# Three k columns of a graph layer's attention moved among its first batches, and three orders in the count sweeps

## Chip, cores and metric

One Trainium2 chip, one core. The metric is the device time of one launch in microseconds, the median of several executions.

## What is computed

Four graph layers over 512 nodes of 512 features and 8704 edges (src, dst, type, weight), each with a residual and a layer norm around it. Two of them are attentions. Layer 0 has a dense score bias with the edge weights; layer 1 is a graph convolution by degree; layer 2 sums messages by relation; layer 3 is attention over the edges:

```python
q = (h @ Wq).reshape(n, H, DK)
k = (h @ Wk).reshape(n, H, DK)
v = (h @ Wv).reshape(n, H, DK)
e = jnp.einsum('ehd,ehd->eh', k[src], q[dst]) / np.sqrt(DK).astype(np.float32)
...
a = jax.ops.segment_sum(attn[:, :, None] * v[src], dst, num_segments=n)
```

with 8 heads of 64. Because there are few nodes, the kernel works with dense 512 x 512 matrices: it counts the edges between each pair of nodes, and an edge that occurs c times enters layer 3's softmax as a bias log c on the dense score.

## The kernel before, in words

**Precision.** Every product of float32 matrices is three products: each operand is split into a high half (`th`, `wh`, `qh`, `kh`, rounded to the matrix format) and a low half (the rest), and low x high, high x low and high x high are added in one PSUM bank (`product`). A result that is needed as an operand is cast by ScalarE (`high`), and VectorE subtracts to get the low half (`part_low`, L1438), which frees the bank. The weights' high halves are DMA copies issued from GpSimd's queue (`cast`, L371; three slots, so a copy waits for the last product with the weight that was in its slot, `W_LAST`); their low halves are GpSimd subtractions (`low`, L379) of a copy that SyncE's queue loads in quarters.

**Count sweeps.** The edges come in 68 chunks of 128. For each chunk VectorE builds one-hot tiles (`build_chunk`: the source, and the destination with a digit for the type) in a ring of four slots, and TensorE multiplies them into eight banks, 8 products of 128 x 512 a chunk (`chunk`, `sweep`). There are two sweeps, of 8 and 9 blocks of 4 chunks. In between, ScalarE copies banks 0 to 3 out and VectorE banks 4 to 7 (L1373), and the second sweep starts each bank with one product (L596) once it is free. From the third block on VectorE also marks duplicate edges: `mark` compares the keys of one chunk with those behind it, `settle` writes the cell of two chunks (`cell_at`), and GpSimd scatters the edge weights of these cells to DRAM (L444). Before the first loop VectorE also computes `second` and splits the bias rows into `add2` (`bias_rows`), between the chunks of its third block. The one-hot tiles are compared with `iota`, a row of numbers that is loaded by ScalarE's queue (L987); the edges `ei` are the first load of SyncE's queue (L299), and VectorE's first wait.

**Attention** (`attention`, one function on each engine, called for layers 0 and 3). An item m of 32 is one head and one of four row tiles. Its steps:
- scores, in banks 0 to 3, two items at a time (TensorE, L670)
- bias added and row peak taken, which frees the score bank (VectorE `peak_of`, L1479)
- exponent with row sum (ScalarE `exponent`, L955), reciprocal of the sum (VectorE `inverse_of`)
- scaling (GpSimd `scale_rows`, L403)
- four transposes of 128 x 128, in banks 4 to 6 (TensorE `probT`, L679)
- copy of the transposed row out of its bank: even items ScalarE (`even_row`), odd items VectorE (`odd_row`)
- the product with v, when all rows of a head pair are there, in bank 7 or 3 (TensorE, L692).

Every queue is written out by hand in batches b = 0 to 8 of four items: batch b on TensorE holds the scores of items 4b to 4b+3, the transposes of items 4b-4 to 4b-1, and then value products. Scores of batch b need the banks that the peaks of batch b-1 free. Head pair p (items 8p to 8p+7) uses column p of q and k: column 1 from batch 2, column 2 from batch 4, column 3 from batch 6. `psum_plan` (L67) gives each result its bank and its turn in it.

**Layer 3 before the attention.** After v, TensorE makes q columns 0 to 3 (banks 0 to 3) and k columns 0 to 3 (banks 4 to 7), 12 products each (L871, L872); ScalarE and VectorE follow with the halves in the same order. GpSimd's queue holds here the low halves of the output weight, then `cast(19)` and `cast(20)` (L510, L511; the two weights of the last feed-forward step), then `scale_rows`, which has the low halves of weights 19 and 20 behind items 4, 7, 10, 13, 16 and 19.

Of the kernel before, what the change touches and what calls it, by code (L numbers as in the profile page):

```python
# [22 lines left out]
ALU = mybir.AluOpType  # L23
# [43 lines left out]
def psum_plan():  # L67
# [47 lines left out]
    tiles("k3", 4)  # L115
# [26 lines left out]
def build(nc, x0, x0t, row_ids_d, edges, edge_rows, edge_w, weights, rows_of, cols_of, rel_b, ident_d, iota_d, later_d, out):  # L142
# [6 lines left out]
    with ExitStack() as ctx:  # L149
# [147 lines left out]
        def _(sp_):  # L297
            eng = sp_
            eng.dma_start(ei[:], edges.rearrange("a p c -> p a c")).then_inc(s["ld_edge"], 16)  # L299
# [68 lines left out]
        def _(pool):  # L368
# [28 lines left out]
            def scale_rows(a, base, mask, work):  # L397

                for m in range(ITEMS):
# [7 lines left out]
                    if a == 0 and m == 11:  # L407
                        cast(5)
# [102 lines left out]
            cast(20)  # L511
# [9 lines left out]
        def _(pe):  # L521
# [103 lines left out]

            def rows(name, w, ready, ks=K):
# [28 lines left out]
            def attention(a, base):  # L655
                first, v_done = 4 * (a // 3), 4 * (a // 3 + 1)
                for b in range(BATCHES + 2):
# [16 lines left out]
                    for t in range(4 * b - 4, 4 * b):  # L674
                        if 0 <= t < ITEMS:
# [195 lines left out]
            columns("q3", 16, lambda i: None)  # L871
            columns("k3", 17, lambda i: None)  # L872
# [43 lines left out]
        def _(act):  # L916
# [33 lines left out]
            def attention(a, base):  # L950
# [16 lines left out]
                for b in range(BATCHES + 1):  # L967
# [8 lines left out]
                    if b:  # L976
                        even_row(4 * b - 2)
                    if b < BATCHES:
                        exponent(4 * b + 2)
                        exponent(4 * b + 3)  # L980
                for p in range(2, HEADS // 2):
                    mixed(a, p)
# [4 lines left out]
            act.dma_start(iota[:], iota_d.to_broadcast([P, 2 * N])).then_inc(s["ld_iota"], 16)  # L987
# [175 lines left out]
            for f in range(K):  # L1163
                high(("q3", f), qh[:, f, :], s["q_high"])
            for f in range(K):
                high(("k3", f), kh[:, f, :], s["k_high2"])
# [33 lines left out]
        def _(dve):  # L1200
# [144 lines left out]
            for slot in range(RING):  # L1345
                dve.wait_ge(s["hot_used1"], FIRST_PLACED * RING + slot - RING + 1)
                build_chunk(FIRST_PLACED * RING + slot, slot)
                if slot == 1:
                    dve.wait_ge(s["ld_ident"], 16)
                    link(dve.tensor_reduce(second[:], ident[:, 1::32], AX_X, ALU.add))  # L1350
                    link(dve.tensor_scalar(second[:], second[:], -1.0, None, ALU.mult))
                if slot == 2:
                    dve.wait_ge(s["ld_bias"], 64)
                    bias_rows(rows[:], slice(0, P), 0)
# [10 lines left out]
            before, behind = CBLOCKS[0] * RING, (CBLOCKS[0] - FIRST_PLACED) * RING  # L1365
            dve.wait_ge(ld_keys[2], 16)
            dve.wait_ge(ld_keys[3], 16)
            for slot in range(RING - 1):
                dve.wait_ge(s["hot_used1"], before - RING + slot + 1)
                build_chunk(before + slot, slot)  # L1370
            for i in range(T):
# [3 lines left out]
            for k in range(GROUP):  # L1375
                mark(behind, k)
                if k % 2:
                    settle(behind, behind // GROUP, k // 2)
# [91 lines left out]
            def attention(a, base):  # L1470
# [26 lines left out]
                for b in range(BATCHES + 1):  # L1497
                    if b:
                        inverse_of(4 * b - 1)
# [372 lines left out]
```

## Time and profile before

| | us |
|---|---|
| median of 3 executions | 529.7 (529.44 to 530.45) |
| profiled execution, its own time | 532.03 |
| its span, first to last instruction | 530.1 |
| TensorE busy in the span | 503.2 |
| VectorE busy | 382.8 |
| GpSimd busy | 277.7 |
| ScalarE busy | 225.7 |

The profile is that of one execution. A row gives the start, the duration, the engine and line, the operation, output and input with their shapes, and in brackets the idle time before it with what ended it. PE is TensorE, DVE VectorE, ACT ScalarE, POOL GpSimd, SP SyncE; a q behind the name is the engine's own queue, where DMAs are issued. Matrix products overlap, so one that lasts 0.39 us is followed by the next after some 0.22 us.

### The profile page before, as it was taken

Reading aid. Unit: us, or ns where it says so; the run is one execution under the profiler, and the core shown is the slowest. Engines: PE = TensorE matmul, PEld = TensorE weight load, DVE = VectorE, ACT = ScalarE, POOL = GpSimd, SP = SyncE. Lnnn points to the kernel's source line nnn. Section 1 sums busy time; section 2 is a strip of 40 time slices with the busy share of each in tenths; the row PEclk is TensorE's granted clock in tenths of the full one; section 3 lists DMA queues with packets and bytes.
Section 4 is the critical chain, followed back from the end, with each engine's and each line's share of the span. In section 5 each row is a group of like instructions: output and inputs, shape, how many; then the busy total and the mean of one; then the engine's idle time right before and its main releaser. Section 6 shows DMA issues by size and latency. Waiting matters only on the chain.

```text
span 530.1 us, 7860 instructions
## 1 busy us (share of the span) xinstructions
PE 503.2 (95%) x2483; PEld 344.5 (65%) x2498; DVE 382.8 (72%) x972; ACT 225.7 (43%) x474; POOL 277.7 (52%) x283
## 2 busy tenths in 40 slices
PE   7999999999999899999999999999999999899992
PEld 2444444444786564787788888889888786565771
DVE  5999979999986776977654863764348625776586
ACT  2102370004614776557461244435535225776365
POOL 5877777777403989402552544523532752867101
PEclk9999999999999999999999999999999998999998
DMA  6923410000293441050853564322453853100002
GB/s 192 354 74 108 113 28 1 0 0 2 85 355 100 133 122 61 4 176 19 246 155 104 183 187 137 124 80 80 131 172 97 254 163 88 52 0 1 2 0 79
DMA packets 32409, 56.48 MB, mean 107 GB/s; under 512 B 5152, under 2 KB 8686, under 8 KB 31864
## 3 DMA queue, kind: packets, MB, share of 16 engines
q1 hardware_dynamic: 19276, 31.35, 19.1%
q0 software_dynamic: 11728, 18.92, 12.0%
q10 hardware_dynamic: 1372, 5.81, 3.0%
q8 instruction: 17, 0.28, 0.2%
q14 instruction: 16, 0.13, 0.1%
HBM read 51.79 MB, written 4.26 MB: 106 GB/s over the span
## 4 chain that ended last, share of the span: by engine, by line
PE 70%; POOL 9%; DVE 7%; issue 6%; DMA 5%; ACT 4%; POOLq 0%; DVEq 0%; ACTq 0%
PE bank L563 12%; PE bank L564 12%; PE bank L565 12%; PE bank L586 11%; PE bank L692 4%; PE bank L783 3%; PE bank L782 3%; POOL wl L389 3%; PE bank L679 3%; DMA edge_bias<-nbias 3%; POOL sp L403 2%; PE bank L670 2%; PE bank L644 2%; POOL edge_bias L444 1%; DVE sp L1479 1%
## 5 line engine op out<-in xcount | busy, mean ns | idle before, releaser
L389 POOL TENSOR_TENSOR wl<-wraw,wh 128x512 fp32r<-128x512 f32 (+1 forms) x78 | 102.1, 1324 | 71.6 <-DMA wh<-w 15.5
L586 PE MATMUL bank<-hot 128*128 128x512 bf16 x514 | 114.3, 379 | 4.3 <-DVE hot L1303 3.4
L586 PEld LDWEIGHTS bank<-hot 128*128 128x128 bf16 x528 | 51.2, 98 | 67.5 <-DVE hot L1303 6.4
L444 POOL DMA_INDIRECT edge_bias<-ew,cell_at x68 | 71.1, 1046 | 30.3 <-issue 17.7
L563 PE MATMUL bank<-wh,tl 128*128 128x512 f32 x176 | 69.5, 395 | 0.1
L565 PE MATMUL bank<-wh,th 128*128 128x512 f32 x176 | 68.8, 391 | 0.0
L564 PE MATMUL bank<-wl,th 128*128 128x512 f32 x176 | 68.7, 390 | 0.0
L1303 DVE TENSOR_SCALAR hot<-iota,pair_dst,digit 128x1024 bf16<-128x1024 f16 x68 | 41.9, 616 | 0.2 <-issue 0.2
L955 ACT ACTIVATE sp<-sp,peak 128x512 f32<-128x512 f32 x44 | 31.8, 723 | 23.6 <-DVE peak L1479 23.2
L1302 DVE TENSOR_SCALAR hot<-iota,ef 128x512 bf16<-128x512 f16 x68 | 37.7, 554 | 4.9 <-PE bank L586 3.9
L1284 DVE SCALAR_TENSOR_TENSOR eq<-keyb,key,later 128x384 f16<-128x384 f16 (+1 forms) x68 | 40.1, 612 | 0.0
L563 PEld LDWEIGHTS bank<-wh,tl 128*128 128x128 f32 x176 | 33.1, 188 | 8.0 <-issue 1.3
L565 PEld LDWEIGHTS bank<-wh,th 128*128 128x128 f32 x176 | 33.0, 188 | 7.1
L564 PEld LDWEIGHTS bank<-wl,th 128*128 128x128 f32 x176 | 33.1, 188 | 6.8
L1206 DVE TENSOR_TENSOR tl<-bank,th 128x512 fp32r<-128x512 f32 x32 | 21.9, 689 | 18.1 <-ACT th L930 11.1
L940 ACT ACTIVATE gap<-h,neg 128x512 f32<-128x512 f32 x24 | 17.4, 726 | 35.9 <-DVE neg L1217 35.9
L563 PE MATMUL bank<-th,wl 128*128 128x512 f32 x80 | 31.2, 390 | 0.7 <-issue 0.7
L564 PE MATMUL bank<-tl,wh 128*128 128x512 f32 x80 | 31.2, 389 | 0.2 <-issue 0.2
L468 POOL TENSOR_SCALAR x<-h,neg,rstd 128x512 f32<-128x512 f32 x6 | 5.5, 924 | 49.2 <-DVE rstd L1266 49.1
L565 PE MATMUL bank<-th,wh 128*128 128x512 f32 x80 | 31.2, 390 | 0.0
L1479 DVE CUSTOM_DVE_ANT_0 sp<-bank,nbias 128x512 f32<-128x512 f32 x44 | 29.4, 682 | 1.3 <-PE bank L670 0.8
L692 PE MATMUL bank<-probT,v 128*64 128x512 f32 x128 | 30.1, 602 | 0.0
(239 smaller groups left out, 1062.1 us busy)
## 6 DMA issues: line engine op xcount, KB each, us to landing
wraw<-w SPq DMA_DIRECT2D x26, 256.0 KB
wh<-w POOLq DMA_DIRECT2D x6, 1024.0 KB, 6.3
keyb<-edge_keys ACTq DMA_DIRECT2D x4, 1088.0 KB, 9.7
wh<-w_rel POOLq DMA_DIRECT2D x4, 1024.0 KB, 5.9
wraw<-w_rel SPq DMA_DIRECT2D x16, 256.0 KB
wraw<-w_qkv SPq DMA_DIRECT2D x8, 256.0 KB
wh<-w_o POOLq DMA_DIRECT2D x2, 1024.0 KB, 6.8
count_rows<-counts SPq DMA_DIRECT2D x1, 2048.0 KB, 14.1
```

The source lines that it names most:

```text
L389: pool.tensor_tensor(wl[n % WSLOTS][:, k, 0:width], wraw[:, q % 3, 0:width], wh[n % WSLOTS][:, k, 0:width], ALU.subtract).then_inc(s["w_lo ...
L444: pool.indirect_dma_start(out=bias_dram, out_offset=bass.IndirectOffsetOnAxis(ap=cell_at[:, c:c + 1], axis=0), in_=ew[:, c:c + 1], in_offs ...
L563: pe.matmul(ps(name)[:], al, bh, start=start and k == 0, stop=False)
L564: pe.matmul(ps(name)[:], ah, bl, start=False, stop=False)
L565: mm = pe.matmul(ps(name)[:], ah, bh, start=False, stop=stop and k == ks - 1)
L586: mm = pe.matmul(ps(name)[:], hot[:, slot, 0, i * P:(i + 1) * P], hot[:, slot, 1 + kind, :], start=False, stop=last, skip_group_check=True)
L692: mm = pe.matmul(ps(name)[HD * e:HD * e + HD, :], v[:, j, hd * HD:(hd + 1) * HD], probT[:, hd % 4, j, :], start=j == 0, stop=j == T - 1, s ...
L955: act.activation(sp[m % SP][:], sp[m % SP][:], ACT.Exp, bias=peak[:, c:c + 1], scale=-1.0, accum_out=total[:, c:c + 1]).then_inc(s["exped" ...
L1284: return dve.scalar_tensor_tensor(out=eq[:, k, :], in0=keyb[:, bass.ds(c * P, WINDOW * P)], scalar=key[:, bass.ds(c, 1)], in1=later[:], op ...
L1302: dve.tensor_scalar(hot[:, slot, 0, :], iota[:, 0:N], ef[:, 0, bass.ds(j, 1)], None, ALU.is_equal)
L1303: dve.tensor_scalar(hot[:, slot, 1:3, :].rearrange("p a n -> p (a n)"), iota[:], pair_dst[:, bass.ds(j, 1)], digit[:, bass.ds(j, 1)], ALU. ...
L1479: frees(dve.tensor_tensor_reduce(sp[m % SP][:], ps(name)[:], nbias[:, item(m)[1], :], -HD ** -0.5, 3e38, ALU.add, ALU.min, peak[:, c:c + 1 ...
```

## The change

In layer 3, q columns 0 to 2 are followed by k column 0 and q column 3. K columns 1 to 3 are made in the attention's batches 0 to 2, on TensorE ahead of the transposes of the batch's third item (in batch 0 there is none: behind the scores), all three in bank 7. ScalarE casts column b+1 behind batch b's four exponents and moves the batch's second row copy behind that; VectorE makes the low half in the next batch, ahead of its peaks, and moves the second row copy behind the fourth peak. `cast(20)` moves from ahead of the scalings to behind the twelfth.

In the sweeps, the load of `iota` moves from ScalarE's queue to the head of SyncE's; `second` and the bias rows move from VectorE's third block to behind its first loop; and the first two marks of the next group, with their settle, move from behind the bank copies to between the second and third build of the second sweep.

```diff
@@ psum_plan
-    tiles("k3", 4)
+    for f in range(K):
+        use(("k3", f), 7 if f else 4)
@@ SyncE, head of the queue
+            eng.dma_start(iota[:], iota_d.to_broadcast([P, 2 * N])).then_inc(s["ld_iota"], 16)
@@ GpSimd, scale_rows
-                    if a == 0 and m == 11:
-                        cast(5)
+                    if m == 11:
+                        cast(5 if a == 0 else 20)
...
             cast(19)
-            cast(20)
@@ TensorE
+            def column(name, w, f):
+                begin((name, f))
+                finish(product((name, f), w_tile(w, f), t_tile()), (name, f))
@@ TensorE, attention
                     for t in range(4 * b - 4, 4 * b):
+                        if a == 3 and t == 4 * b - 2 and b < K - 1:
+                            column("k3", 17, b + 1)
@@ TensorE, layer 3
-            columns("q3", 16, lambda i: None)
-            columns("k3", 17, lambda i: None)
+            w_ready(16)
+            for f in range(K - 1):
+                column("q3", 16, f)
+            w_ready(17)
+            column("k3", 17, 0)
+            column("q3", 16, K - 1)
@@ ScalarE, attention
-                    if b:
+                    beside = a == 3 and b < K - 1
+                    if b and not beside:
                         even_row(4 * b - 2)
                     if b < BATCHES:
                         exponent(4 * b + 2)
                         exponent(4 * b + 3)
+                    if beside:
+                        high(("k3", b + 1), kh[:, b + 1, :], s["k_high2"])
+                        if b:
+                            even_row(4 * b - 2)
...
-            act.dma_start(iota[:], iota_d.to_broadcast([P, 2 * N])).then_inc(s["ld_iota"], 16)
@@ VectorE, attention
                         inverse_of(4 * b - 1)
+                    if a == 3 and 0 < b < K:
+                        part_low("k3", b, kl, kh, 0.0, s["k_high2"], s["k_ready"])
...
-                    if b:
+                    beside = a == 3 and b < K - 1
+                    if b and not beside:
                         odd_row(4 * b - 1)
                     if b < BATCHES:
                         peak_of(4 * b + 3)
                         inverse_of(4 * b + 2)
+                    if b and beside:
+                        odd_row(4 * b - 1)
@@ VectorE, sweeps
                 build_chunk(FIRST_PLACED * RING + slot, slot)
-                if slot == 1:
-                    dve.wait_ge(s["ld_ident"], 16)
-                    link(dve.tensor_reduce(second[:], ident[:, 1::32], AX_X, ALU.add))
-                    link(dve.tensor_scalar(second[:], second[:], -1.0, None, ALU.mult))
-                if slot == 2:
-                    dve.wait_ge(s["ld_bias"], 64)
-                    bias_rows(rows[:], slice(0, P), 0)
@@ VectorE, behind the first loop
+            dve.wait_ge(s["ld_ident"], 16)
+            link(dve.tensor_reduce(second[:], ident[:, 1::32], AX_X, ALU.add))
+            link(dve.tensor_scalar(second[:], second[:], -1.0, None, ALU.mult))
+            dve.wait_ge(s["ld_bias"], 64)
+            bias_rows(rows[:], slice(0, P), 0)
             dve.wait_ge(ld_keys[2], 16)
             dve.wait_ge(ld_keys[3], 16)
             for slot in range(RING - 1):
                 dve.wait_ge(s["hot_used1"], before - RING + slot + 1)
                 build_chunk(before + slot, slot)
+                if slot == 1:
+                    mark(behind, 0)
+                    mark(behind, 1)
+                    settle(behind, behind // GROUP, 0)
...
             build_chunk(before + RING - 1, RING - 1)
-            for k in range(GROUP):
-                mark(behind, k)
-                if k % 2:
-                    settle(behind, behind // GROUP, k // 2)
+            mark(behind, 2)
+            mark(behind, 3)
+            settle(behind, behind // GROUP, 1)
```

Layer 3's halves of q and k on ScalarE and VectorE outside the attention follow TensorE's new order (q 0 to 2, k 0, q 3).

## Rows read from the trace of the kernel before

**Rows 1.** The page's first part: busy time, share of the span and instructions.

```profile
PE 503.2 (95%) x2483; PEld 344.5 (65%) x2498; DVE 382.8 (72%) x972; ACT 225.7 (43%) x474; POOL 277.7 (52%) x283
```

**Rows 2.** TensorE's timeline, 0 to 84 us: start, duration, what, idle before it.

```profile
7.06 12.26 PE L586 MATMUL bank<-hot 128*128 128x512 bf16 x55 [1.37 <-DVE hot L1303]
...
29.46 34.71 PE L586 MATMUL bank<-hot 128*128 128x512 bf16 x155 [0.67 <-DVE hot L1303]
...
66.33 13.98 PE L586 MATMUL bank<-hot 128*128 128x512 bf16 x63
81.34 2.98 PE L586 MATMUL bank<-hot 128*128 128x512 bf16 x12 [1.03 <-DVE hot L1303]
```

**Rows 3.** TensorE's timeline in layer 3's attention.

```profile
441.47 0.50 PE L670 MATMUL bank<-kh,ql 64*128 64x512 f32 x2
...
447.56 3.15 PE L679 MATMUL bank<-ident,sp 128*128 128x128 f32 x16
...
455.36 0.63 PE L679 MATMUL bank<-ident,sp 128*128 128x128 f32 x4 [0.70 <-ACT probT L964]
...
462.91 0.50 PE L670 MATMUL bank<-kh,ql 64*128 64x512 f32 x2
...
464.49 2.21 PE L679 MATMUL bank<-ident,sp 128*128 128x128 f32 x16
466.64 1.94 PE L692 MATMUL bank<-probT,v 128*64 128x512 f32 x8
```

**Rows 4.** Busy time by stretch; behind it granted clock, DMA share, GB/s.

```profile
447.60:456.00 8.40, 7.28 (x47) 5.81 (x46) 6.30 (x23) 6.41 (x16) 5.71 (x8) 0.86 0.08 19
```

**Rows 5.** ScalarE's timeline, the casts of k columns 2 and 3.

```profile
438.86 0.59 ACT L925 CAST kh<-bank 128x512 fp32r<-128x512 f32 x1 [2.13 <-PE bank L565]
441.58 0.59 ACT L925 CAST kh<-bank 128x512 fp32r<-128x512 f32 x1 [2.13 <-PE bank L565]
```

**Rows 6.** VectorE's timeline, last low half of k and first peak.

```profile
442.20 0.69 DVE L1441 SCALAR_TENSOR_TENSOR kl<-bank,kh 128x512 fp32r<-128x512 f32 x1 [2.03 <-ACT kh L925]
443.15 0.69 DVE L1479 CUSTOM_DVE_ANT_0 sp<-bank,nbias 128x512 f32<-128x512 f32 x1 [0.26 <-DVE kl L1441]
```

**Rows 7.** GpSimd's timeline, weight copies and first scalings of layer 3.

```profile
436.17 0.76 POOL L377 DMA_DIRECT2D wh<-w  x1
...
445.01 1.53 POOL L403 TENSOR_SCALAR sp<-sp,scale,deg 128x512 f32<-128x512 f32 x2 [2.47 <-DVE scale L1486]
```

**Rows 8.** The page's sixth part: weight copies, KB each, us to landing.

```profile
wh<-w POOLq DMA_DIRECT2D x6, 1024.0 KB, 6.3
```

**Rows 9.** Timelines of SyncE's queue and VectorE, the first load.

```profile
0.80 0.43 SPq L299 DMA_DIRECT2D ei<-edges_in  x1
...
4.91 0.27 DVE L1275 CAST ef<-ei 128x204 f32<-128x204 int32 x1 [4.91 <-DMA ei<-edges_in]
```

**Rows 10.** VectorE's timeline, operations of the bias rows.

```profile
22.38 0.15 DVE L1350 TENSOR_REDUCE second<-ident 128x1 f32<-128x4 f32 x1
...
23.49 0.51 DVE L1338 CAST add<-rows 128x512 fp32r<-128x512 f32 x1
24.04 0.75 DVE L1340 SCALAR_TENSOR_TENSOR add<-add,second,rows 128x512 fp32r<-128x512 f32 x1
```

**Rows 11.** Timelines of VectorE and GpSimd between the count sweeps.

```profile
58.08 1.84 DVE L1302 TENSOR_SCALAR hot<-iota,ef 128x512 bf16<-128x512 f16 x1
...
60.38 0.34 DVE L1302 TENSOR_SCALAR hot<-iota,ef 128x512 bf16<-128x512 f16 x1
...
63.56 2.48 DVE L1373 COPY packed<-bank 128x512 f32<-128x512 f32 x4 [0.27 <-PE bank L586]
...
67.84 0.61 DVE L1284 SCALAR_TENSOR_TENSOR eq<-keyb,key,later 128x384 f16<-128x384 f32 x1
...
58.48 1.29 POOL L389 TENSOR_TENSOR wl<-wraw,wh 128x512 fp32r<-128x512 f32 x1
```

**Rows 12.** VectorE's timeline in the second sweep's first rounds.

```profile
79.95 0.86 DVE L1302 TENSOR_SCALAR hot<-iota,ef 128x512 bf16<-128x512 f16 x1 [3.31 <-PE bank L586]
```

More of the change, by code:

```diff
@@ L1162, in _ @@
             turned(3, 3)
-            for f in range(K):
+            for f in range(K - 1):
                 high(("q3", f), qh[:, f, :], s["q_high"])
-            for f in range(K):
-                high(("k3", f), kh[:, f, :], s["k_high2"])
+            high(("k3", 0), kh[:, 0, :], s["k_high2"])
+            high(("q3", K - 1), qh[:, K - 1, :], s["q_high"])
             attention(3, ITEMS)
@@ L1765, in _ @@
             bias_rows(par[0:2, 4, :], slice(0, 2), 2)
-            for f in range(K):
+            for f in range(K - 1):
                 part_low("q3", f, ql, qh, 0.0, s["q_high"], s["q_ready"])
-            for f in range(K):
-                part_low("k3", f, kl, kh, 0.0, s["k_high2"], s["k_ready"])
+            part_low("k3", 0, kl, kh, 0.0, s["k_high2"], s["k_ready"])
+            part_low("q3", K - 1, ql, qh, 0.0, s["q_high"], s["q_ready"])
             attention(3, ITEMS)
```

## The prediction

> **What bounds the kernel now.** I read the page first: TensorE is busy 95% of the span [rows 1]. So the time is TensorE's work plus the places where it stands still or runs slower, and a change of order can win only those. Then I read TensorE's own timeline in the two places that the change touches. In the count sweeps it runs from 7.06 us; two stops are worth looking at, 0.67 us at 29.46 and 1.03 us at 81.34, each ended by a one-hot tile from VectorE [rows 2]. Between the sweeps the merged piece that begins at 29.46 lasts until 64.17, and the second sweep's products begin at 66.33, 2.2 us later, where eight start-up products of the sweep rate (12.26 us / 55 = 0.22 us each) need 1.8.
>
> The larger place is layer 3's attention. The reader is to see how a batch goes when nothing is late: scores at 462.91, transposes at 464.49, value products at 466.64 to 468.5 [rows 3]; that is 1.58, 2.15 and 1.87 us, 5.6 us in all, with TensorE never idle. The first four batches are not like that. Scores of batch 0 begin right after the last k column, 441.47, and batch 4's begin at 462.91: 21.4 us. The work in it is four times 1.58, three times 2.15 and once 1.87: 14.6 us. So **6.8 us are lost there**: waits for a score bank, waits like the 0.70 us for a copied transposed row, and one stretch at the lower of TensorE's two levels [rows 3]. For that last one: the granted clock is 0.86 between 447.6 and 456 [rows 4], after the engine had stood and stuttered from 442.9 on; the 16 transposes at 447.56 took 3.15 us where those at 464.49 took 2.21, so it cost about 0.9.
>
> **Part 1, the k columns in the attention.** A column is 12 products; the casts that follow two columns start 2.72 us apart [rows 5]. Three columns, 8.16 us of TensorE work, leave the stretch before the attention and enter batches 0 to 2. Nothing is added to TensorE. The attention begins 8.16 us earlier, at 433.3. If TensorE were never idle, batch 4 would begin at 433.3 + 14.6 + 8.2 = 456.1. I followed the four queues through the new order with the durations in [rows 3, 5, 6], and found these delays:
> - q column 3 is now the last one before the scores, and it sits in the bank that score 3 takes. Its cast (0.59 us) and its low half (0.69) stand before that score: first pair of scores 433.3 to 434.1, second from 434.7. Lost: 0.6.
> - Column 1 runs 435.5 to 438.2. VectorE and ScalarE do the first four peaks and exponents meanwhile, 8.16 us earlier than before. Scores 4 to 7 follow without a wait, transposes of items 0 and 1 until 440.9, column 2 until 443.6, items 2 and 3 until 444.7, scores 8 to 11, items 4 and 5 until 447.3, column 3 until 450.1.
> - The low half of column 1 must have freed bank 7 before column 2: VectorE ends it near 440.2, for 440.9. For column 3: 446.3, for 447.3. Both fit by 0.7 to 1 us. Each half costs VectorE 0.95 us (from 442.20 to the next peak at 443.15) and ScalarE 0.59 [rows 6, 5]; a batch on VectorE is then four peaks and two copies at 0.69 or less and a half, 6 × 0.69 + 0.95 = 5.1 us, beside 6.4 us of TensorE. The postponed copies (items 2 and 6 on ScalarE, 3 and 7 on VectorE) are due only when TensorE comes back to their bank, after the column.
> - Batch 3 keeps one wait of 0.6 to 0.7 us for a copied row. Batch 4 then begins at about 457.4, **5.5 us earlier than 462.91**. From there the kernel is as before; the tail after it depends on nothing older.
> - GpSimd: its queue holds the weight copy of 436.17 (0.76 us), done at 436.93; the first scaling, at 445.01 before, is due 8.16 us earlier, at 436.85 [rows 7]. That fits. The other weight copy (cast 20) waits for k column 3 and is moved to behind the twelfth scaling, 452.9, with no scaling waiting long behind it; its halves are needed from the seventeenth scaling on, near 461, against a landing 6.3 us after the issue [rows 8]. Cost nothing; without this cover a late landing would stop the scalings for as long as it is late.
>
> **Part 2, the iota load.** It goes from ScalarE's queue to the head of SyncE's, so the edge load, issued at 0.80 with 0.43 us of issue, goes out some 0.48 later; VectorE's first operation waits for it at 4.91 and TensorE's first product at 7.06 waits for VectorE [rows 9, 2]. Bounds: nothing, if the load lands no later because the other one has left the engines, and 0.5. I take **+0.4** because the issue is on the path. Every other SyncE load moves too: keys and transposed x have microseconds to spare.
>
> **Part 3, the bias rows and marks.** Two small operations of 0.15, the cast of 0.51 and the product of 0.75 leave the stretch before VectorE's third block [rows 10]: 1.6 us earlier for the tile whose absence stopped TensorE 0.67 us. **−0.7**. They return after the first sweep's loop, together with two marks of 0.61 [rows 11] and a settle, 1.3 us, ahead of the copies that free four banks. VectorE left its loop at 60.3 and would now at 59.1 (−1.6 + 0.4); 1.6 of bias, three builds of some 0.75 (0.34 for the half at 60.38, its other half has twice the columns) and 1.3 of marks bring the copies to 64.2, against 63.56 before [rows 11]. The loop's last build took 1.84 us beside a GpSimd subtraction [rows 11]; if VectorE now passes ahead of that, the copies start when the banks are full, about 63.3. So the second sweep starts between 66.1 and 67.0, was 66.33; I take 66.6, as the build that escapes leaves another one to be held. Against the earlier finish of sweep 1 (−0.3 by the two numbers above) this step costs **+0.5**.
>
> The Trainium skill ("SBUF — State Buffer", Who interferes with whom) says that a VectorE instruction with two SBUF inputs is blocked whole while a GpSimd instruction that reads SBUF runs. By it the moved marks and the bias product could themselves be held for one subtraction; the rows show only builds held, and the sum above does not use it.
>
> After the copies VectorE now has two marks less: 1.3 us more lead into the second loop. TensorE's 1.03 us stop at 81.34 came after VectorE sat 3.31 us and took its next build at 79.95 [rows 12]. I cannot name what ended those 3.31 us (the tile's slot was free long before by the order of the products). Bounds: 0 if the same event comes at the same moment, −1.0 if it moves with VectorE. I take **−0.5**.
>
> **Sum**: −5.5 + 0.4 − 0.7 + 0.5 − 0.5 = −5.8 us. The profiled execution took 532.03 us (span 530.1), 2.3 above the median of 529.7, so part of its stops may be its own: the differences are taken from it, the level from the median. 529.7 − 5.8 = **523.9 us**.
>
> **The rivals.**
> - *The lower clock stays* (0.12). By the granted clock the engine fell after a second of standing and stutter; the 0.6 us stop before the second pair of scores remains. If TensorE's lower level comes again it now falls on dense work: 3.4 us at half rate cost 1.7 instead of 0.9, and the 0.9 counted as gained is not: 523.9 + 1.7 = 525.6. Against it: 0.6 us is a shorter stop than the one before it was, and the columns fill what follows.
> - *The marks are held too* (0.10): as the build at 58.08 was [rows 11], for one subtraction of 1.29 us at the moment of transition, and the 81 us stop stays: 523.9 + 1.3 + 0.5 = 525.7. This is where the rule of the skill named above would decide.
> - *The waits in the sweeps go for good* (0.15): load free, copies on time, stop gone: 523.9 − 0.4 − 0.5 − 0.5 = 522.5.
> - *The halves become the chain* (0.03, the slower side). VectorE's half waits in order for ScalarE's cast, which stands behind four exponents; behind it stand the next peaks. If TensorE comes back to scores before those peaks are done, in each of the three batches, the columns are added instead of hidden: +8.2 put back, 3 × (0.59 + 0.95) for the halves and +0.5 at the transition: 529.7 + 4.6 + 0.5 = 534.8. It decides once peak 7 ends after 445.5, where its bank is wanted for score 11; my walk has it at 443.9, so it lacks 1.6 us.
> - That the change does not act: not possible, every queue's order is written out.
>
> **How the numbers follow.** The forecast as it stands 0.60. The range takes in the clock and held-marks cases and the bounds of the unknown steps (0.4, 0.5, 0.5 each way) and 0.7 for my walk: 522.1 to 526.3. A measurement of this kernel tells about 0.2%, 1.1 us: faster by more 0.95 (all cases but the last, less a little), within 0.02, slower 0.03.
>
> **What would show it.** Right: batch 4's scores 24.1 us behind the end of the last column made before the attention (it was 21.4 with no column in it, and 29.6 if none were hidden); casts of k columns 1 to 3 between exponents; TensorE's clock 1.00 from 440 to 480; no 0.67 stop near 29 us; first sweep product near 7.5. Wrong: a wait of TensorE for a low half of k ahead of columns 2 or 3, GpSimd's scalings late behind a weight copy, a stop over 1 us between the sweeps.

## The result, and the profile of the changed kernel

| | before | after |
|---|---|---|
| median (range) of 7 executions, us | 529.86 (529.44 to 530.45) | 527.01 (525.9 to 528.27) |
| profiled execution, its own time | 532.03 | 527.14 |
| its span | 530.1 | 525.2 |

The ratio is 0.9943, with a 95% interval of 0.993 to 0.9956: faster by 2.85 us. Forecast were 5.8 us and a time of 523.9 with a range of 522.1 to 526.3; the measured time lies 0.7 us above that range. The two profiled executions differ by 4.9 us, more than the medians, because the one of before was 2.2 us slower than its own median.

TensorE's busy time is nearly that of before [rows 1]. From the first part of the page of the changed kernel:

```profile
PE 501.5 (95%) x2483; PEld 343.5 (65%) x2498; DVE 386.5 (74%) x972; ACT 224.7 (43%) x474; POOL 277.5 (53%) x283
```

**The attention went as forecast.** TensorE's timeline of the changed kernel in layer 3's attention (answers to [rows 3]; L670, L679 and L692 are now L676, L687 and L700):

```profile
433.93 0.50 PE L676 MATMUL bank<-kh,ql 64*128 64x512 f32 x2
...
435.40 0.49 PE L676 MATMUL bank<-kh,ql 64*128 64x512 f32 x1 [0.28 <-DVE ql L1458]
...
440.82 1.09 PE L687 MATMUL bank<-ident,sp 128*128 128x128 f32 x8
441.67 0.48 PE L564 MATMUL bank<-th,wl 128*128 128x512 f32 x1
...
455.60 0.63 PE L687 MATMUL bank<-ident,deg_rows 128*128 128x128 f32 x4 [0.75 <-ACT probT L976]
...
458.02 0.50 PE L676 MATMUL bank<-kh,ql 64*128 64x512 f32 x2
```

From the first score to batch 4 are 458.02 - 433.93 = 24.09 us, with three columns in it (24.1 forecast); it was 462.91 - 441.47 = 21.44 us with none [rows 3]. Column 2 begins at 441.67, right behind the eighth transpose, and nothing of k is waited for. The casts stand behind the exponents, on ScalarE's timeline (answers to [rows 5]):

```profile
439.41 0.56 ACT L937 CAST kh<-bank 128x512 fp32r<-128x512 f32 x1
...
445.24 0.56 ACT L937 CAST kh<-bank 128x512 fp32r<-128x512 f32 x1
```

The granted clock is 1.00 where it was 0.86 [rows 4]. Busy time by stretch, with the clock behind the five engines:

```profile
64.00:68.00 4.00, 1.75 (x6) 0.55 (x6) 3.96 (x11) 3.74 (x7) 2.35 (x2) 0.95 0.55 119
68.00:72.00 4.00, 4.00 (x14) 1.42 (x12) 1.93 (x8) 3.90 (x7) 3.10 (x3) 0.62 0.26 66
...
440.00:460.00 20.00, 19.25 (x128) 14.00 (x125) 15.51 (x48) 13.22 (x33) 13.30 (x18) 1.00 0.23 61
```

**The handover between the sweeps did not.** The row of 68 to 72 us is the other news: just behind the handover TensorE is busy all the time but gets 14 products done in 4 us, at a clock of 0.62. In the kernel before, the same stretch is

```profile
68.00:72.00 4.00, 4.00 (x20) 1.81 (x19) 3.77 (x15) 3.90 (x7) 2.49 (x3) 1.00 0.25 66
```

TensorE's timeline there in the changed kernel (answers to [rows 2]; in such a view the last piece ends where the view ends, here at 92 us, so its duration means nothing):

```profile
6.72 12.26 PE L587 MATMUL bank<-hot 128*128 128x512 bf16 x55 [1.03 <-DVE hot L1319]
19.34 43.63 PE L587 MATMUL bank<-hot 128*128 128x512 bf16 x194 [0.36 <-DVE hot L1319]
62.80 1.27 PE L597 MATMUL bank<-offset,minus 128*128 128x512 bf16 x4
65.70 0.39 PE L597 MATMUL bank<-offset,minus 128*128 128x512 bf16 x1 [1.62 <-DVE packed L1391]
66.30 0.39 PE L597 MATMUL bank<-offset,minus 128*128 128x512 bf16 x1 [0.21 <-DVE packed L1391]
66.90 0.39 PE L597 MATMUL bank<-offset,minus 128*128 128x512 bf16 x1 [0.21 <-DVE packed L1391]
67.49 0.55 PE L597 MATMUL bank<-offset,minus 128*128 128x512 bf16 x1 [0.21 <-DVE packed L1391]
67.84 24.39 PE L587 MATMUL bank<-hot 128*128 128x512 bf16 x102
```

The stop of 0.67 us near 29 is gone, the one at 81 too (a profile below shows that the kernel before has executions without them as well), and the first sweep's products end at 19.34 + 43.63 = 62.97 instead of 64.17. But the four start-up products that need VectorE's banks come one by one behind its copies, and the second sweep starts at 67.84, 1.5 us later than before. VectorE's timeline says why (answers to [rows 11] and [rows 10]):

```profile
57.72 2.32 DVE L1319 TENSOR_SCALAR hot<-iota,pair_dst,digit 128x1024 bf16<-128x1024 f16 x1
...
60.03 0.15 DVE L1376 TENSOR_REDUCE second<-ident 128x1 f32<-128x4 f32 x1
...
61.53 0.35 DVE L1318 TENSOR_SCALAR hot<-iota,ef 128x512 bf16<-128x512 f16 x1
...
62.97 0.61 DVE L1300 SCALAR_TENSOR_TENSOR eq<-keyb,key,later 128x384 f16<-128x384 f32 x1
...
64.24 0.35 DVE L1318 TENSOR_SCALAR hot<-iota,ef 128x512 bf16<-128x512 f16 x1
...
64.96 2.48 DVE L1391 COPY packed<-bank 128x512 f32<-128x512 f32 x4
```

and GpSimd's:

```profile
58.46 1.29 POOL L391 TENSOR_TENSOR wl<-wraw,wh 128x512 fp32r<-128x512 f32 x1
```

The durations are the forecast ones: bias rows 1.50 us, two builds 1.44, marks and settle 1.27, one build 0.72. What is wrong is where they begin. VectorE was to leave the loop at 59.1; it left at 60.03, hardly ahead of before (60.38). In the kernel before, the build L1302 took 1.84 us for 0.34 and ended just behind the subtraction of 58.48 to 59.77 [rows 11]; now the next operation, L1319, takes 2.32 us for 0.54 and ends just behind the same subtraction, 58.46 to 59.75.

This was the last of three such meetings. By the starts of the same builds in both timelines VectorE was 1.97 us ahead of before ahead of the subtraction at 45 us (41.16 and 43.13), 1.30 behind it (48.50 and 49.80), 0.68 behind the one at 52 (55.80 and 56.48) and 0.35 behind the one at 58. Beside each of the three, one VectorE operation took 1.8 to 2.3 us in either kernel (now a mark of 2.20 at 44.84 and a build of 2.18 at 51.30), whichever of them VectorE had come to. It also sat 0.49 us at 43.6 to 44.1, waiting for TensorE to free a slot.

### The profile page after: what moved, and what is told of

Same layout as the page of the kernel before. It is cut to its first block, busy times and chain, and to the rows that moved or that the text cites. A ratio compares the mean times of both kernels' runs of the same rounds, so it can differ in the third digit from the quotient of the medians.

```text
span 525.2 us, 7860 instructions
## 1 busy us (share of the span) xinstructions
PE 501.5 (95%) x2483; PEld 343.5 (65%) x2498; DVE 386.5 (74%) x972; ACT 224.7 (43%) x474; POOL 277.5 (53%) x283
## 2 busy tenths in 40 slices
DMA packets 32409, 56.48 MB, mean 108 GB/s; under 512 B 5152, under 2 KB 8686, under 8 KB 31864
## 4 chain that ended last, share of the span: by engine, by line
PE 77%; DVE 10%; POOL 6%; issue 3%; ACT 3%; DMA 1%; DVEq 0%; SPq 0%; POOLq 0%
PE bank L587 17%; PE bank L564 12%; PE bank L566 12%; PE bank L565 12%; PE bank L700 4%; PE bank L687 3%; PE bank L791 3%; PE bank L790 3%; POOL sp L405 2%; PE bank L676 2%; POOL wl L391 2%; DVE hot L1319 2%; PE bank L650 2%; DVE hot L1318 1%; DVE x L1255 1%
## 5 line engine op out<-in xcount | busy, mean ns | idle before, releaser
L587 PE MATMUL bank<-hot 128*128 128x512 bf16 x514 | 115.5, 383 | 2.2 <-DVE hot L1319 1.4
L446 POOL DMA_INDIRECT edge_bias<-ew,cell_at x68 | 72.7, 1069 | 30.4 <-issue 16.7
L1319 DVE TENSOR_SCALAR hot<-iota,pair_dst,digit 128x1024 bf16<-128x1024 f16 x68 | 46.3, 681 | 0.0
L1300 DVE SCALAR_TENSOR_TENSOR eq<-keyb,key,later 128x384 f16<-128x384 f16 (+1 forms) x68 | 41.5, 631 | 0.0
L1318 DVE TENSOR_SCALAR hot<-iota,ef 128x512 bf16<-128x512 f16 x68 | 33.4, 491 | 4.2 <-PE bank L587 3.7
L700 PE MATMUL bank<-probT,v 128*64 128x512 f32 x128 | 30.1, 602 | 0.0
```

The costliest lines, as they stand in the source:

```text
L446: pool.indirect_dma_start(out=bias_dram, out_offset=bass.IndirectOffsetOnAxis(ap=cell_at[:, c:c + 1], axis=0), in_=ew[:, c:c + 1], in_offs ...
L587: mm = pe.matmul(ps(name)[:], hot[:, slot, 0, i * P:(i + 1) * P], hot[:, slot, 1 + kind, :], start=False, stop=last, skip_group_check=True)
L700: mm = pe.matmul(ps(name)[HD * e:HD * e + HD, :], v[:, j, hd * HD:(hd + 1) * HD], probT[:, hd % 4, j, :], start=j == 0, stop=j == T - 1, s ...
L1300: return dve.scalar_tensor_tensor(out=eq[:, k, :], in0=keyb[:, bass.ds(c * P, WINDOW * P)], scalar=key[:, bass.ds(c, 1)], in1=later[:], op ...
L1318: dve.tensor_scalar(hot[:, slot, 0, :], iota[:, 0:N], ef[:, 0, bass.ds(j, 1)], None, ALU.is_equal)
L1319: dve.tensor_scalar(hot[:, slot, 1:3, :].rearrange("p a n -> p (a n)"), iota[:], pair_dst[:, bass.ds(j, 1)], digit[:, bass.ds(j, 1)], ALU. ...
```

## The experiments

All but two, which repeat a kernel with no edit, are edits of the changed kernel or of the kernel before in those parts that the change touches. Each median is compared with that of the kernel before on the same chip: 529.98 for the first four, 529.93 for the next four, 529.62 for the last four. Three short diffs against the changed kernel undo one part each, and are called by their names below:

```diff
 iota back (SyncE's queue, then ScalarE's)
-            eng.dma_start(iota[:], iota_d.to_broadcast([P, 2 * N])).then_inc(s["ld_iota"], 16)
...
+            act.dma_start(iota[:], iota_d.to_broadcast([P, 2 * N])).then_inc(s["ld_iota"], 16)
 bias back (third block, then behind the loop)
+                if slot == 1:
...
+                if slot == 2:
+                    dve.wait_ge(s["ld_bias"], 64)
+                    bias_rows(rows[:], slice(0, P), 0)
...
-            bias_rows(rows[:], slice(0, P), 0)
 marks back (from ahead of the four copies to behind them)
-                if slot == 1:
-                    mark(behind, 0)
-                    mark(behind, 1)
-                    settle(behind, behind // GROUP, 0)
...
             build_chunk(before + RING - 1, RING - 1)
+            mark(behind, 0)
+            mark(behind, 1)
+            settle(behind, behind // GROUP, 0)
             mark(behind, 2)
```

### The kernel before, once more

No edit.

> The kernel before once more, for a second profile of it. Theory H (handover: the marks and bias rows between the sweeps cost the rest of the gain) says nothing new of it: 529.9 us. Theory B (the profiled execution of before was 2.2 us over its own median, so some of the losses read from it are not in the usual execution) expects a span of about 528 with either no stop of 1.03 us near 81 us or no lower clock in layer 3's first batches, and 24.5 us or less between the end of k column 3 and batch 4's scores minus what is missing: 20.5 instead of 21.4.

Measured: 530.16, ratio 0.9998 (0.9983 to 1.0012). TensorE's timeline of this execution (530.39 us, near the median) has none of the stops of [rows 2]:

```profile
7.05 57.11 PE L586 MATMUL bank<-hot 128*128 128x512 bf16 x249 [1.36 <-DVE hot L1303]
...
66.31 17.86 PE L586 MATMUL bank<-hot 128*128 128x512 bf16 x80
```

From 4 to 12 us it made fewer products than the execution of [rows 2] in the same busy time, 20 against 27, as at the lower level; the clock column gives 1.00 for both, so only the count of products says it. That this is what left VectorE ahead, and so no stop, is my reading and was not tried. All seven profiles of versions with the bias rows in their old place fit it: the four that made 26 to 28 products from 4 to 12 us have the stop near 29, the three that made 18 to 20 do not.

All the same the second sweep starts at 66.31, as at 66.33 there: the stop near 29 costs nothing. The stop at 81 us did cost where it came: the 15 products that end the counting (L613) begin at 126.24 there and at 125.02 here. But it stands near 81 us in only two of the fourteen profiles of all versions, so it is not part of a median execution. Layer 0's first score comes at 161.32 where it came at 163.82, so the profile shown of before was a slow one by what happened between 66 and 164 us.

Theory B's last sign did not come. From the first score of layer 3 to batch 4 are 461.25 - 439.17 = 22.08 us, more than the 21.44 of [rows 3], at a granted clock of 0.69 from 440 to 451 us (0.84 there). How long this stretch of the kernel before takes depends on how much of it runs at the lower level.

### The attention alone

Iota, bias and marks back.

> The k columns alone, the sweeps as before. Theory H: the whole -5.5 us, 524.4 us, and batch 4's scores 24.1 us behind the first score. Theory B: the gain is smaller in the usual execution, -3 to -4 us, 526 to 527 us, though the stretch of the attention is as long as in the changed kernel.

Measured: 524.63 (524.43 to 525.22), ratio 0.9902 (0.9886 to 0.9918), 5.35 us faster. First score 431.39, batch 4 455.48: again 24.09 us. At the handover TensorE is as before, with seven start-up products in one piece:

```profile
64.25 1.92 PE L596 MATMUL bank<-offset,minus 128*128 128x512 bf16 x7
66.34 0.39 PE L596 MATMUL bank<-offset,minus 128*128 128x512 bf16 x1 [0.18 <-DVE packed L1389]
66.57 25.63 PE L586 MATMUL bank<-hot 128*128 128x512 bf16 x115
```

What follows: the k columns are worth the 5.5 us that were forecast for them, within the noise, and the three orders in the sweeps together cost 2.4 us (527.01 - 524.63).

### The sweeps' three orders alone

The kernel before, with only those parts of the change that lie in the count sweeps.

> The three orders of the sweeps alone, layer 3 as before. Theory H: slower than before by 1.5 to 2.5 us (the copies of banks 4 to 7 start near 65 instead of 63.6, TensorE stands 2.2 us and runs at the lower clock for 3.4 us behind that), 531.4 to 532.4 us. Theory B: within 0.5 us of before.

Measured: 533.45 (532.35 to 534.83), ratio 1.0069 (1.0051 to 1.0087), 3.5 us slower, 1 us above the range expected. The second sweep starts at 68.17, and the clock falls here too:

```profile
65.98 0.39 PE L597 MATMUL bank<-offset,minus 128*128 128x512 bf16 x1 [1.67 <-DVE packed L1375]
```

```profile
64.00:68.00 4.00, 1.92 (x5) 0.44 (x6) 3.96 (x11) 3.73 (x6) 2.44 (x3) 0.87 0.71 149
68.00:72.00 4.00, 4.00 (x14) 1.58 (x13) 2.34 (x8) 3.90 (x7) 2.24 (x3) 0.70 0.23 66
```

So the loss is at the handover and needs nothing of the attention. Lost at the lower level: 4 x (1 - 0.87) + 4 x (1 - 0.70) = 1.7 us. By layer 0's first score the loss is the same as in the changed kernel: 164.35 against 161.32 in the profile above, 164.47 against 161.53 with and without the orders beside the k columns, 3.0 and 2.9 us. The medians give 3.5 and 2.4; what makes them differ is open.

In this execution the clock stayed at 1.00 in the attention (441 to 464 us), and the stretch to batch 4 takes 463.53 - 443.01 = 20.52 us, 0.92 less than the 21.44 of [rows 3]. That is the 0.9 us that the prediction gave to the lower level there.

### Marks back; marks and bias back; bias back

Three edits that leave the attention as changed: marks back alone, marks and bias back (only the iota load stays moved), and bias back alone.

> The changed kernel with the two marks and their settle behind the copies again. Theory H: the copies start 1.3 us earlier, at 63.6, TensorE stands 0.9 us less and the clock may stay at 1.00: 1.3 to 2.5 us faster than the changed kernel, 524.5 to 525.7 us. Theory B: as the changed kernel, 527.0 us.

> The k columns and the load of iota on SyncE's queue; bias rows and marks as before. Theory H puts the whole loss on the work ahead of the bank copies, so this is as fast as the k columns alone, 524.6 us, or up to 0.3 less (in two profiles with the moved load the first product came 0.1 to 0.3 us earlier than in those of before). Rival I: part of the loss is the moved load (every other load of SyncE's queue goes out 0.4 us later), 525 to 526 us.

> The changed kernel with the bias rows in the third block again; the two marks stay ahead of the copies. Theory H: the copies start about 1 us earlier than in the changed kernel (64.0 instead of 65.0), TensorE stands some 0.5 us more than before and the clock stays: 525 to 525.5 us. Rival M: the marks ahead of the copies are harmful in any case, as in the changed kernel, 527 us.

Measured: 524.63 (0.9904, 0.9888 to 0.992), 524.62 (0.9914, 0.9895 to 0.9933) and 524.91 (0.9911, 0.9896 to 0.9926). Each undoes the whole loss, to 0.3 us. The timelines of TensorE, marks back first, then bias back:

```profile
66.61 25.63 PE L587 MATMUL bank<-hot 128*128 128x512 bf16 x115
```

```profile
66.11 0.39 PE L597 MATMUL bank<-offset,minus 128*128 128x512 bf16 x1 [0.21 <-DVE packed L1393]
66.71 0.39 PE L597 MATMUL bank<-offset,minus 128*128 128x512 bf16 x1 [0.21 <-DVE packed L1393]
66.94 25.42 PE L587 MATMUL bank<-hot 128*128 128x512 bf16 x114
```

The bias rows alone behind the loop (1.5 us) and the marks alone ahead of the copies (1.3 us) fit into the slack that VectorE has; both together do not. Before, the slack can be read directly: VectorE waits 0.27 us for a full bank ahead of its copies [rows 11], is idle 0.58 us ahead of the build before that, and TensorE comes to the banks copied by VectorE only after four start-up products of its own:

```profile
62.48 0.35 DVE L1302 TENSOR_SCALAR hot<-iota,ef 128x512 bf16<-128x512 f16 x1 [0.58 <-issue]
```

The iota load by itself changes nothing that can be measured.

### Bias rows behind the copies

Marks back, and the bias rows on VectorE behind the four copies and the last build, ahead of the marks.

```diff
             build_chunk(before + RING - 1, RING - 1)
+            dve.wait_ge(s["ld_ident"], 16)
...
+            bias_rows(rows[:], slice(0, P), 0)
+            mark(behind, 0)
```

> Marks behind the copies as before, and the bias rows behind the copies and the build after them, where VectorE sat 2 us in the changed kernel's profile. Theory H: nothing stands ahead of the copies, sweep 1's stop before its third block is gone and the copies start when the banks are full: 523.9 to 524.6 us, the fastest version if it is at the lower end. Rival C (where TensorE's level comes up late, at 10 us as in two of six profiles, nothing is gained by the missing stop): 524.6 us.

Measured: 524.89, ratio 0.9911 (0.9895 to 0.9926), no better than leaving them where they were, so the hoped-for 523.9 did not come. Its profiled execution was the slowest of six, 526.12, and has a stop at 81 us again (0.51 us), behind a build that took 2.25 us. Its time differs from the others' by less than the executions differ among themselves, so it says no more than that the place costs nothing.

### All four marks ahead of the copies

A doubled dose of the suspected cost: the other pair of marks and their settle follow the first pair, ahead of the copies.

```diff
                     settle(behind, behind // GROUP, 0)
+                    mark(behind, 2)
+                    mark(behind, 3)
+                    settle(behind, behind // GROUP, 1)
...
-            mark(behind, 2)
-            mark(behind, 3)
-            settle(behind, behind // GROUP, 1)
```

> The dose doubled: all four marks and both settles ahead of the copies. Theory H: the copies start 1.3 us later than in the changed kernel, at 66.3, and TensorE stands 1.3 us longer: 528.3 us, more if the lower clock lasts longer. Rival (the loss comes from where the work behind the copies went, not from the copies): 527.0 us or less, since VectorE then has 1.3 us more lead into its second loop.

Measured: 530.49 (529.42 to 531.4), ratio 1.0014 (1.0003 to 1.0024): 3.5 us above the changed kernel, for 1.3 us of marks, and 2.2 above what was expected. VectorE's, GpSimd's and TensorE's timelines, and the stretches:

```profile
64.86 0.16 DVE L1313 SCALAR_TENSOR_TENSOR cell_at<-dup,key 128x2 uint32<-128x2 f32 x1
...
66.13 1.58 DVE L1313 SCALAR_TENSOR_TENSOR cell_at<-dup,key 128x2 uint32<-128x2 f32 x1
...
68.35 2.47 DVE L1394 COPY packed<-bank 128x512 f32<-128x512 f32 x4
```

```profile
66.41 1.28 POOL L391 TENSOR_TENSOR wl<-wraw,wh 128x512 fp32r<-128x512 f32 x1
```

```profile
69.09 2.40 PE L597 MATMUL bank<-offset,minus 128*128 128x512 bf16 x4 [3.71 <-DVE packed L1394]
71.29 21.00 PE L587 MATMUL bank<-hot 128*128 128x512 bf16 x92
```

```profile
68.00:72.00 4.00, 2.91 (x6) 0.74 (x7) 3.54 (x7) 2.87 (x5) 2.39 (x3) 0.62 0.24 66
```

A settle of two columns took 0.16 us the first time and 1.58 the second, beside the subtraction; its row begins 0.28 us ahead of the subtraction's, and the two end within 0.02 us of each other. The copies come 68.35 - 64.96 = 3.4 us later than in the changed kernel: 1.3 for the work moved, 1.4 for the settle that was held, and 0.7 because this execution was that much later already at the first settle (64.86 instead of 64.16). TensorE stands 3.71 us, and the whole time follows. The Trainium skill ("SBUF — State Buffer", Who interferes with whom) says that a VectorE instruction with two SBUF inputs waits out a GpSimd instruction that reads SBUF; this settle has two such inputs, and the trace agrees with 1.58 us for 0.16 us of work.

### The standing filled with products, beside the changed kernel once more

TensorE repeats the start-up product of bank 3 eight times while it would wait for bank 4. Each starts the bank anew with the same values, so nothing else changes. The second run is the changed kernel with no edit.

```diff
                     pe.matmul(ps(name)[:], minus[:], offset[:], start=True, stop=False, skip_group_check=True)
+                    if w == 2 and name == names[3]:
+                        for _ in range(8):
+                            pe.matmul(ps(name)[:], minus[:], offset[:], start=True, stop=False, skip_group_check=True)
```

> The changed kernel, with eight more start-up products into bank 3 (each writes the same values again) between the start-ups of banks 3 and 4 of the second sweep: 1.8 us of TensorE work in the place where it stands 1.6 us for the first bank copy. Theory K (the loss behind the standing is the lower clock, and it falls because TensorE stands): the clock stays at 1.00 at 68 us and the kernel is 1.3 to 1.7 us faster than the changed one, 525.4 to 525.8 us, though it does more work. Rival S (only the late copies cost, the clock falls anyway): 527.0 to 527.3 us, lower clock still there.

> The changed kernel once more, beside the filled one: 527.0 us, copies of the banks from 65 us, clock 0.5 for 3.4 us or more between 66 and 75 us.

Measured: 525.82 (525.48 to 526.0), ratio 0.9929 (0.9915 to 0.9942), against 527.01 (525.98 to 528.73), ratio 0.9958 (0.9942 to 0.9974). TensorE with the filling, and its clock:

```profile
64.73 1.89 PE L600 MATMUL bank<-offset,minus 128*128 128x512 bf16 x8
...
67.69 24.55 PE L587 MATMUL bank<-hot 128*128 128x512 bf16 x113
```

```profile
68.00:72.00 4.00, 4.00 (x20) 1.76 (x19) 3.25 (x12) 3.90 (x7) 3.08 (x4) 1.00 0.26 66
```

and without it, in the fastest of its executions:

```profile
66.10 0.39 PE L597 MATMUL bank<-offset,minus 128*128 128x512 bf16 x1 [0.61 <-DVE packed L1391]
...
68.12 24.12 PE L587 MATMUL bank<-hot 128*128 128x512 bf16 x111
```

```profile
68.00:72.00 4.00, 4.00 (x19) 1.76 (x18) 3.29 (x12) 3.90 (x7) 2.69 (x3) 1.00 0.27 66
```

In this execution the start-up products began later (64.22 instead of 62.80), TensorE stood 0.61 instead of 1.62 us, and the clock stayed at 1.00; the second sweep still starts at 68.12, because VectorE's copies set that moment. So the lower clock expected at 66 to 75 us did not show in this profile, and the filled profile alone proves little: its start-up products began at 63.62, and unfilled it would have stood an estimated 0.8 us (63.62 + 1.27 to some 65.7, 0.74 behind the start of the copies at 64.93, as in the changed kernel). What speaks for the filling is the set of executions. It leaves the start as late (67.69) and takes 1.2 us off the median; its five executions lie within 0.5 us where the six unfilled ones spread over 2.75; and the mean granted clock of a whole execution is 0.994 or 0.995 in all five, but 0.990 to 0.996 in the thirteen executions of the changed kernel. The intervals of the two ratios just touch.

So the loss has two parts: the late copies in every execution, 525.82 - 524.62 = 1.2 us against the kernel with only the iota load moved beside the k columns (0.8 by the two ratios, as they ran on different chips), and the lower clock, 1.2 us in the median. It costs up to 1.7 us where it comes, and does not come in each. The traces show both parts at layer 0's first score: 161.53 for the k columns alone, 162.75 filled, 163.09 unfilled with the clock at 1.00, and 164.47 in the first profile of the changed kernel, where it fell.

### Another bank for q column 3

The sweeps as in the kernel before but for the iota load; q column 3 goes to bank 5, which no score needs.

```diff
-    tiles("q3", 0)
+    for f in range(K):
+        use(("q3", f), 5 if f == K - 1 else f)
```

> The k columns and the iota load, and q column 3 in bank 5 instead of bank 3, so that score 3 needn't wait for its low half. By the first item of the prediction's part 1 this gives back 0.6 us: 524.0 us, and batch 4's scores 23.5 us behind the first score. Rival: the peaks of items 2 and 3 and the exponents set the pace and nothing is gained, 524.6 us.

Measured: 524.09 (523.38 to 524.71), ratio 0.9892 (0.9877 to 0.9908): the fastest version that was run, by 0.5 us, though its range overlaps that of the next. What TensorE waits for from 425 to 490 us, in all, how often and the longest, no longer has the wait for `ql`:

```profile
PE bank L688 <- ACT probT L977: 0.7, 1, 0.7
PE bank L688 <- POOL sp L406: 0.3, 1, 0.3
```

The stretch from the first score to batch 4 is now 455.22 - 431.60 = 23.62 us, 0.47 less than 24.09.

### The columns ahead of the batch's first transposes

Again with the sweeps of before but for the iota load.

```diff
-                        if a == 3 and t == 4 * b - 2 and b < K - 1:
+                        if a == 3 and t == 4 * b - 4 and b < K - 1:
```

> The k columns and the iota load, each column ahead of the first transposes of its batch instead of between the second and third. If TensorE's own work is the bound, the place hardly matters: column 2 then waits 0.3 to 0.5 us for bank 7 (its low half is ready near the end of scores 7) and the rest is the same, 524.6 to 525.1 us. If the place matters because the transposes feed the copies that free the banks, 1 us or more slower, 525.6 us and up.

Measured: 528.71 (528.3 to 529.41), ratio 0.9981 (0.997 to 0.9991). Of the two expectations the second holds, and with a larger number: the place is worth 4 us. From the same view of TensorE's waits:

```profile
PE bank L687 <- ACT probT L976: 1.8, 2, 1.5
PE bank L564 <- DVE kl L1459: 1.1, 1, 1.1
...
```

The wait for bank 7 comes ahead of column 3 (446.87), which wants the bank before VectorE has taken the low half of column 2; column 2 itself waits for nothing. The stretch to batch 4 takes 459.75 - 431.88 = 27.87 us instead of 24.09. Of these 3.8 us, 2.2 are in the waits of this view (3.5 in all instead of 1.3), among them 1.45 us for one copied row at 457.33; where the rest goes, and whether the late column or the transposes left without a column between them cost more, was not separated.

## Why the prediction was wrong, and where it was right

**Part 1, the k columns (-5.5): right.** Alone they gave 5.35 us, in the 24.1 us forecast, at a clock of 1.00. Some luck is in the number, since the forecast took the stretch of before from one execution: 21.44 us there, 22.08 in another, 20.52 in one whose clock stayed up, so against 24.09 - 8.16 = 15.93 us the same change is worth 4.6 to 6.2 us by these three. The delays that the walk through the queues had found are there: that for q's low half ahead of the second pair of scores (0.28 us of waiting in the row, 0.47 by the run with another bank, 0.6 forecast), 0.75 for a copied row in batch 3, nothing for k. The halves fitted, as forecast; the run with the columns two items earlier shows that they fit by little (1.1 us of waiting). GpSimd was no later than before: TensorE waits once for a scaled row, 0.3 us, in both kernels.

**Part 2, the iota load (+0.4): nothing.** The edge load is issued 0.44 us later, but VectorE's first cast came at 4.55 to 4.89 us in the eleven profiles with the load moved, and at 4.91 [rows 9], 4.89 and 5.15 in the three without: no later. The median with and without it is the same (524.62 and 524.63). The lower bound given was the true one.

**Part 3, the orders in the sweeps (-0.7, +0.5, -0.5, in sum -0.7): this is the step that failed**, and it failed in sign. Measured is +2.4. Four things were wrong in it.
- *The start of the chain.* The forecast carried the 1.6 us that VectorE saves in its third block to the end of the loop. They did not arrive: it left at 60.03, not 59.1. The lead shrank beside each of three GpSimd subtractions, from 1.97 us to 1.30, 0.68 and 0.35. The prediction had the row of a held build at the last of them, and took it as something that VectorE might escape by coming earlier; it did not look for the others.
- *The handover itself (+0.5).* From copies at 64.2, its own sum, the prediction had bounds of 66.1 to 67.0 for the second sweep and took 66.6, for a build that escapes; its sum stood for the upper bound. With the right start the same sum gives 60.03 + 1.50 + 1.44 + 1.27 + 0.72 = 64.96 for the copies, as measured, and the second sweep begins four copies of 0.6 us and some 0.4 us later, at 67.84 instead of 66.6. What TensorE stands was left out of the forecast; it is 1.62 us and three times 0.21.
- *The clock.* No term had it at this place; the rival that the lower level comes back was set in the attention. The row of 68 to 72 us shows 0.62, and with the row before it (0.95) this is 4 x 0.38 + 4 x 0.05 = 1.7 us.
- *The two gains (-0.7, -0.5)* were stops of one execution. They did go, and nothing came of it. The first sweep did end 1.2 us earlier in the trace, but the second starts when VectorE's copies are done and not when TensorE is. The stop at 81 us is absent from a second profile of the kernel before as well. The prediction had the warning in it (the profiled execution 2.3 us above its median) and took both differences from that execution nevertheless.

With what was measured the sum is -5.35 for the attention, +1.2 for the late copies, +1.2 for the clock, 0 for the rest, -2.95 against the -2.85 of the result. The terms are differences of neighbouring medians, so that they close is no test of its own; what supports them is the traces, in which the start of the second sweep and the clock show the two losses apart.

**The rivals.** *The lower clock stays* and *the marks are held too* both named times near the result's (525.6 and 525.7), for other reasons than the true one: the clock fell, but between the sweeps; the marks ran their 0.61 us each unheld in the changed kernel, and a settle was held only when all marks were put there (and a mark in the first loop, 2.20 us at 44.84, where no one had priced it). *The sweeps' waits go for good* and *the halves become the chain* did not come. The sign that would have shown the forecast wrong, a stop over 1 us between the sweeps, is what the trace shows.

## What to carry to other kernels

At a handover where several engines wait for one another, work out when each is ready, and do not price a move by the work moved: here 1.3 us or 1.5 us alone cost 0.3 us at most, 2.8 us cost 2.4, and 4.1 us cost 5.9 (530.49 against 524.62). Time that an engine saves early arrives later only if nothing in between takes it away, such as another engine's instruction that holds it. Look for every such instruction on the way, not only for the last. And take a stop in the profile of one execution for a gain only if it lies on what the median does; one more profile of the same kernel shows which stops stay.

## What was unexpected of the hardware

- A stand of 1.6 us at the handover was followed by TensorE's lower level (1.2 GHz), which cost 1.7 us, more than the stand. A stand of 0.61 us plus three of 0.21 was not. With eight repeated products in the gap the median fell by 1.2 us, and the one profile taken shows the level kept.
- A settle of 128 x 2 elements took 1.58 us beside a GpSimd subtraction instead of 0.16, and ended with it. The smallest operation here lost as much as the large ones: 1.4 us, against 1.5 for a build of 128 x 512 [rows 11].
- Two executions of one kernel can differ in the stops of a whole sweep and leave it at the same moment: the stops at 19 and 29 us (0.37 and 0.67) stood in one profile of the kernel before and in the other not, and both started the second sweep at 66.3.
